# Graph attention, layer 1: the tile's sum enters each group's aggregation through an identity product, ScalarE copies it back, VectorE rescales, four message buffers

## What is computed

```python
h = (x @ W).reshape(n, NHEAD, OUT_FEATS)
h_l = (a_l * h).sum(-1)
h_r = (a_r * h).sum(-1)
e = h_l[row] + h_r[col]
e = jnp.where(e > 0, e, ALPHA * e)
m = jax.ops.segment_max(e, row, num_segments=n)
ex = jnp.exp(e - m[row])
denom = jax.ops.segment_sum(ex, row, num_segments=n)
att = ex / (denom[row] + 1e-16)
msg = att[:, :, None] * h[col]
out = jax.ops.segment_sum(msg, row, num_segments=n)
```

## Time and profile before

| | us |
|---|---|
| median of 3 runs | 2386.41 |
| lowest, highest | 2377.89, 2386.74 |
| span of the profiled execution | 2383.0 |

### The profile page before, as it was taken

How to read it: one execution, slowest core, us unless ns; L and a number is a source line. 1 busy time by engine, 2 the same in 40 slices (tenths; PEclk the granted TensorE clock), 3 DMA queues, 4 the chain that set the end, 5 groups by cost and what they waited for, 6 DMA issues and landing times.

```text
span 2383.0 us, 44547 instructions
## 1 busy us (share of the span) xinstructions
PE 1942.2 (82%) x9758; PEld 1420.1 (60%) x9759; DVE 1818.7 (76%) x4333; ACT 1484.5 (62%) x5321; POOL 1484.6 (62%) x1468
## 2 busy tenths in 40 slices
PE   0889999999928889888898899855778787878774
PEld 0457777777716777677777677632445454545442
DVE  7873333333348999999999999785889998999987
ACT  2236666666617777777778777446666666666660
POOL 3737777777777666666566656127666666666660
PEclk9999999999968999999999999987998989898997
DMA  8343333333329898888889885025434334343311
GB/s 238 127 179 131 131 131 129 131 131 130 123 92 328 291 298 292 300 295 297 297 287 304 302 292 174 4 60 133 106 105 106 105 105 107 99 112 100 108 37 54
DMA packets 162160, 403.34 MB, mean 169 GB/s; under 512 B 46887, under 2 KB 59099, under 8 KB 162108
## 3 DMA queue, kind: packets, MB, share of 16 engines
q0 software_dynamic: 79360, 276.09, 35.9%
q1 hardware_dynamic: 82748, 126.67, 16.8%
HBM read 343.89 MB, written 84.72 MB: 180 GB/s over the span
## 4 chain that ended last, share of the span: by engine, by line
PE 36%; DVE 25%; issue 15%; DMA 9%; POOL 7%; DVEq 3%; ACT 3%; ACTq 0%; SPq 0%; POOLq 0%
PE ps L1421 12%; DMA arena<-sorted_edges 6%; POOL sorted_edges L570 5%; PE ps L1454 4%; DVE gmx L1273 4%; PE ps L1457 4%; PE ps L1407 4%; PE ps L1469 3%; DVE arena L1305 2%; PE ps L1579 2%; DVE work L1268 2%; DVEq L334 2%; DVE arena L1102 2%; DVE sc L1116 2%; DMA arena<-node_row,idxC 2%
## 5 line engine op out<-in xcount | busy, mean ns | idle before, releaser
L639 POOL DMA_INDIRECT arena<-node_row,idxC x464 | 484.4, 1044 | 238.5 <-issue 132.6
L570 POOL DMA_INDIRECT sorted_edges<-work,idxA x416 | 417.3, 1003 | 146.7 <-issue 143.9
L1062 DVE TENSOR_TENSOR work<-ps,b_bc 128x512 f32<-128x512 f32 x208 | 143.9, 692 | 322.9 <-PE ps L1421 322.9
L1421 PE MATMUL ps<-w_sb,arena 128*128 128x256 f32 x1664 | 386.7, 385 | 0.0
L1579 PE MATMUL ps<-arena,hq 128*128 128x260 f32 x928 | 282.2, 432 | 86.5 <-DVE work L1268 81.1
L1421 PEld LDWEIGHTS ps<-w_sb,arena 128*128 128x128 f32 x1664 | 307.6, 190 | 72.0 <-issue 34.3
L594 POOL DMA_INDIRECT work<-node_kvx,idxB x232 | 244.5, 1054 | 156.6 <-DVE arena L1133 51.6
L594 POOL DMA_INDIRECT arena<-node_kvx,idxB x232 | 240.9, 1038 | 144.2 <-issue 53.4
L709 ACT ACTIVATE work<-work 128x256 f32<-128x256 f32 x416 | 188.7, 500 | 193.3 <-DVE work L1062 193.3
L1273 DVE TENSOR_REDUCE gmx<-ps 128x4 f32<-128x1024 f32 x232 | 283.1, 1220 | 31.5 <-PE ps L1554 31.5
L1454 PE MATMUL ps<-arena,work 128*128 128x256 f32 x928 | 255.6, 399 | 59.5 <-issue 40.6
(11 more groups left out here) (195 smaller groups left out, 3868.1 us busy)
## 6 DMA issues: line engine op xcount, KB each, us to landing
arena<-sorted_edges SPq DMA_DIRECT2D x232, 260.0 KB, 4.7
work<-sorted_rows SPq DMA_DIRECT2D x58, 256.0 KB, 3.5
arena<-in_edge_attr SPq DMA_DIRECT2D x25, 512.0 KB, 3.6
node_kvx<-arena SPq DMA_DIRECT2D x24, 384.0 KB, 2.3
arena<-node_row,idxC POOLq DMA_INDIRECT x464, 2.9
sorted_edges<-work,idxA POOLq DMA_INDIRECT x416, 2.4
sorted_edges<-arena SPq DMA_DIRECT2D x25, 260.0 KB
sorted_edges<-arena SPq DMA_DIRECT2D x1, 6240.0 KB
```

What stands on the lines that cost most here:

```text
L570: pool.indirect_dma_start(rec_dram[:, :], bass.IndirectOffsetOnAxis(ap=idxA[:, st.slot(8), c:c + 1], axis=0), recA[:, st.slot(8), c, :], N ...
L639: pool.indirect_dma_start(row1_g[:, st.slot(16), j, :], None, row1_dram[:, :], bass.IndirectOffsetOnAxis(ap=idxC[:, batch(st).slot(4), st. ...
L1421: ins = pe.matmul(ps[:, 5 + t, half * H:(half + 1) * H], hidT[:, r, m, half, t * P:(t + 1) * P], w2_sb[:, m, :], start=m == 0, stop=m == 1)
```

## The change

The tile's sum no longer meets the group's sum on VectorE. TensorE adds a third product to the group's aggregation, the identity times the tile's sum, in the same PSUM bank, so that the bank holds the new sum; ScalarE copies the bank to `acc1`. VectorE keeps only the rescaling, once in four groups. TensorE aggregates group s - 14 at step s, ScalarE copies group s - 15 at step s, and VectorE rescales for group s - 10. The message ring grows from two to four, with a semaphore of its own (`msg1_used`) that is set ahead of the identity product. TensorE and ScalarE now also read the tile numbers, twice in a turn each.

```diff
@@ scalar
                     act.copy(hrT[0:PARTS, pair(c).slot(2), :], trh).then_inc(s("hrT"), 1)
+                if st.u % 8 == 0:
+                    act_tiles[15] = tiles16(ACT_ENGINE, st.k, 15, st.u // 8)
+                d = st.back(15)
+                if d.real():
+                    act.wait_ge(s("agg1_ready"), d.n + 1)
+                    act.copy(acc1[:, bass.ds(act_tiles[15][st.u % 8], 1), :].rearrange("p a n -> p (a n)"),
+                             agg1[d.slot(2)]).then_inc(s("acc1_done"), 1)
...
-                        act.wait_ge(s("agg1_ready"), st.n - 15)
+                        act.wait_ge(s("msg1_used"), st.n - 15)
@@ vector
-                c = st.back(11)
-                if c.real():
-                    acc = tile(acc1, tiles[8][st.u % 8])
+                c = st.back(10)
+                if c.real() and c.u % BG == 0:
+                    acc, k = tile(acc1, tiles[10][st.u % 8]), batch(c)
+                    dve.wait_ge(s("mscale"), k.n + 1)
                     if not c.first(1):
                         dve.wait_ge(s("acc1_done"), c.n)
...
-                    dve.wait_ge(s("agg1_ready"), c.n + 1)
-                    dve.tensor_tensor(acc, acc, agg1[c.slot(2)], ALU.add).then_inc(
-                        s("acc1_done"), 1)
...
-                if st.u == 7:
-                    tiles[8] = tiles16(DVE, st.k, 11, 1)
+                if st.u % 8 == 0:
+                    tiles[10] = tiles16(DVE, st.k, 10, st.u // 8)
...
-                    if not m.first(2):
-                        dve.wait_ge(s("agg1_ready"), m.n - 1)
-                    dve.tensor_tensor(msg1[:, m.slot(2), :, :].rearrange("p c (h d) -> p c h d", d=HE),
+                    if not m.first(4):
+                        dve.wait_ge(s("msg1_used"), m.n - 3)
+                    dve.tensor_tensor(msg1[:, m.slot(4), :, :].rearrange("p c (h d) -> p c h d", d=HE),
@@ tensor
-                d = st.back(13)
+                if st.u % 8 == 0:
+                    pe_tiles[14] = tiles16(PE, st.k, 14, st.u // 8)
+                d = st.back(14)
                 if d.real():
...
                     for j in range(GJ):
-                        ins = pe.matmul(agg1[r], oneh1[:, r16, j, :], msg1[:, r, j, :],
-                                        start=j == 0, stop=j == GJ - 1)
-                    ins.then_inc(s("agg1_ready"), 1)
+                        ins = pe.matmul(agg1[r], oneh1[:, r16, j, :], msg1[:, r4, j, :],
+                                        start=j == 0, stop=False)
+                    ins.then_inc(s("msg1_used"), 1)
+                    if d.u % BG == 0:
+                        pe.wait_ge(s("acc1_scaled"), batch(d).n + 1)
+                    else:
+                        pe.wait_ge(s("acc1_done"), n)
+                    pe.matmul(agg1[r], ident[:, :],
+                              acc1[:, bass.ds(pe_tiles[14][st.u % 8], 1), :].rearrange("p a n -> p (a n)"),
+                              start=False, stop=True).then_inc(s("agg1_ready"), 1)
@@ gpsimd
-            pool.memset(hrT[:, :, :], 0.0).then_inc(s("acc1_zero"), 1)
             pool.wait_ge(s("acc0_done"), NG)
+            pool.memset(hrT[:, :, :], 0.0).then_inc(s("acc1_zero"), 1)
```

More of the change, by code:

```diff
@@ L256, in gnn_kernel @@
         row1_g = carve(16 * GJ * ROW1).rearrange("p (s c n) -> p s c n", s=16, c=GJ)
-        msg1 = carve(2 * GJ * NH1 * HE).rearrange("p (s c n) -> p s c n", s=2, c=GJ)
+        msg1 = carve(4 * GJ * NH1 * HE).rearrange("p (s c n) -> p s c n", s=4, c=GJ)
         hrT = carve(2 * 2 * GJ * P // 2).bitcast(BF16).rearrange("p (s n) -> p s n", s=2)
@@ L606, in _ @@
             pool.memset(gmx[:, :, :, 0:1], -BIG).then_inc(s("acc1_zero"), 1)
+            pool.wait_ge(s("acc0_done"), NG)
             pool.memset(hrT[:, :, :], 0.0).then_inc(s("acc1_zero"), 1)
-            pool.wait_ge(s("acc0_done"), NG)
             for r in range(4):
@@ L887, in layer1 @@
                     act.activation(mscale[:, r, :], mdiff[:, r, :], ACT.Exp).then_inc(s("mscale"), 1)
-            run(act, NG, 16, 9, layer1)
+            run(act, NG, 16, 15, layer1)
         @block.vector
@@ L1251, in layer1 @@
                 g, b = st.u % BG, batch(st)
-                if st.u == 0:
-                    tiles[8] = tiles16(DVE, st.k, 11, 0)
-                c = st.back(11)
-                if c.real():
-                    acc = tile(acc1, tiles[8][st.u % 8])
+                c = st.back(10)
+                if c.real() and c.u % BG == 0:
+                    acc, k = tile(acc1, tiles[10][st.u % 8]), batch(c)
+                    dve.wait_ge(s("mscale"), k.n + 1)
                     if not c.first(1):
                         dve.wait_ge(s("acc1_done"), c.n)
[L1259 to L1266, removed]
-                    dve.wait_ge(s("agg1_ready"), c.n + 1)
-                    dve.tensor_tensor(acc, acc, agg1[c.slot(2)], ALU.add).then_inc(
-                        s("acc1_done"), 1)
+                    dve.tensor_tensor(acc.rearrange("p (h d) -> p h d", d=HE),
+                                      acc.rearrange("p (h d) -> p h d", d=HE),
+                                      mscale[:, k.slot(2), :].unsqueeze(2).to_broadcast([P, NH1, HE]),
+                                      ALU.mult).then_inc(s("acc1_scaled"), 1)
                 if st.real():
@@ L1310, in layer1 @@
                     top(b, st)
-            run(dve, NG, 16, 11, layer1)
+            run(dve, NG, 16, 10, layer1)
             dve.wait_ge(s("acc1_done"), NG)
@@ L1569, in layer1 @@
                     ins.then_inc(s("hm_mm"), 1)
-                d = st.back(13)
+                if st.u % 8 == 0:
+                    pe_tiles[14] = tiles16(PE, st.k, 14, st.u // 8)
+                d = st.back(14)
                 if d.real():
-                    n, r, r16 = d.n, d.slot(2), d.slot(16)
+                    n, r, r16, r4 = d.n, d.slot(2), d.slot(16), d.slot(4)
                     pe.wait_ge(s("oneh1"), n + 1)
@@ L1578, in layer1 @@
                     for j in range(GJ):
-                        ins = pe.matmul(agg1[r], oneh1[:, r16, j, :], msg1[:, r, j, :],
-                                        start=j == 0, stop=j == GJ - 1)
-                    ins.then_inc(s("agg1_ready"), 1)
-            run(pe, NG, 16, 13, layer1)
+                        ins = pe.matmul(agg1[r], oneh1[:, r16, j, :], msg1[:, r4, j, :],
[8 more added lines that the diff above has]
+                              start=False, stop=True).then_inc(s("agg1_ready"), 1)
+            pe_tiles = {}
+            run(pe, NG, 16, 14, layer1)
 def run8(eng, total, body):
```

## The result

The changed kernel takes 2503.4 us (median of four runs, 2502.8 to 2509.5) against 2384.4 us before (four runs): the ratio is 1.0505, with a 95% interval of 1.0485 to 1.0525. It is 119 us slower; the prediction had 2513 us, 127 us slower.

A forecast was written before the change was run, and what follows sets the result against it. VectorE bounds the kernel before; afterwards a chain between ScalarE and TensorE does. Turns of 58.4 against 49.75 us, x 14.5, give 125 us, plus 2 for the drain: 127 us more, 2513 us, range 2400 to 2600.

The forecast's parts named there:

- if nothing else came late: VectorE's own work falls from 49.75 to some 42 us a turn; with no other delay the gain would be 109 us.
- The ring: TensorE's step s - 2, ScalarE's copy, one-hot and L853, TensorE's step s wait in turn: two passages, 12.40 us a batch.
- first passage: Into step 4k: identity product's end, ScalarE's copy, one-hot, mask, L853, then TensorE's step to its product's end: 7.47 us.
- second passage: Into step 4k + 2, the same way without the mask: 2.09 on ScalarE, 0.16, 2.68 on TensorE, 4.93 us.
- table reads, a turn: Tile-number reads, twice a turn: 1.9 us each on TensorE, nothing more on ScalarE, 3.8 us a turn.
- clock, a turn: TensorE idles 2.4 us a batch and its clock then halves: 1.2 us lost a batch, 4.8 a turn.
- a turn: 16 groups, four batches: 53.6 us with table reads and loop, 58.4 with the clock loss, against 49.75 before.
- the turn's head: The loop's own time in each turn of 16 groups: 0.2 us.
- The rescaling: VectorE stands ahead of L1262 for ScalarE's copy, 2 to 3 us a batch, which it has to spare: covered.
- (a): Ring holds but TensorE's clock stays up or its loss is covered: turn 53.6 us, +58 us, 2444 us; chance 0.28.
- (b): ScalarE's queue is less late, next busiest engine sets the pace: turn 46.2 us, -51 us, 2335 us; chance 0.12.
- Buys nothing then: The message ring of four brings no gain after the change, since the wait isn't at VectorE.

The follow-up runs named there:

- the fastest kernel: ScalarE's copy and VectorE's rescaling each one step later, against the changed kernel: 2354.4 us, ratio 0.9871 to the kernel before.

## Why the prediction was right

**The bound before.** VectorE set the pace: shortening its addition alone gave 35 us. But something else was nearer behind it than the 109 us of "if nothing else came late" would need.

**The ring.** This is the cause. The order of instructions in ScalarE's queue (49 us for moving the copy behind the one-hot), the work in that queue (71 us against 8 for the same instruction after and before) and the lag of the copy (73 us) all move the time, and none of the three changes TensorE's amount of work. The terms, at full clock, in us:

| term | predicted | measured |
|---|---|---|
| product's end to L853's end, first passage | 4.42 | 4.44 |
| ScalarE to TensorE | 0.16 | 0.05 |
| TensorE's step 4k | 2.89 | 2.97 |
| first passage | 7.47 | 7.46 |
| second passage | 4.93 | 4.85 |
| a batch | 12.40 | 12.31 |
| table reads, a turn | 3.8 | 2.7 |
| clock, a turn | 4.8 | 4.5 |
| a turn | 58.4 | 58.11 |

The measured turn is the distance from the L1536 at 2069.77 to the one 16 groups earlier:

```profile
2011.66 0.59 PE L1536 MATMUL ps<-ident_b,arena 128*12 128x128 bf16 x4 [2.79 <-ACT arena L853]
...
2027.12 0.39 PE L1536 MATMUL ps<-ident_b,arena 128*12 128x128 bf16 x4 [2.31 <-ACT arena L853]
...
2041.10 0.38 PE L1536 MATMUL ps<-ident_b,arena 128*12 128x128 bf16 x4 [2.38 <-ACT arena L853]
```

Its four batches take 15.46, 13.98, 15.87 and 12.80 us. It is a typical one: ten turns from the L1536 at 1750.29 us to the one at 2331.23 take 58.09 us each. The last batch has full clock and no read: 12.31, and 0.48 for the turn's head, by which the hole at 2069.77 is longer (2.79 against 2.31); I had 0.2 for that head. (58.11 - 49.75) x 14.5 = 121 us, against 119 measured.

The clock and read terms in the table come from experiments that take each away alone, and so they don't add up: 49.2 + 0.5 + 2.7 + 4.5 = 56.9 leaves 1.2 us a turn. Taken one after the other they come closer. At full clock a turn should be 49.2 + 0.5 + 2.8 for the reads = 52.5, and with the hole filled it is 53.06; from there to 58.09 the clock takes 5.0. (The 4.5 is less, as it spreads the gain over the first turn too, whose holes were not filled.) About 0.5 us a turn stays without a name.

That the turn came out within 0.3 us is partly luck. The reads were 1.0 too high and the head 0.3 too low; within the first passage the time from product to copy was 0.14 and not 0.04, and the time from ScalarE to TensorE 0.05 and not 0.16. The order of the instructions, both passages and the size of the clock's loss were not luck.

**The clock.** Taking 15 of 19 holes as marked was close: of the 47 holes of 2.1 to 2.8 us ahead of L1536 between 1766 and 2431 in the changed kernel, 38 had the clock at 0.5 within two us of them. The 9 others all stand ahead of the fourth batch of a turn. The granted clock was to be "at or below 0.90", and is 0.85.

**The rescaling.** I had called it covered, with VectorE at rest 2 to 3 us a batch, which is what the trace shows (73.9 us in 32 waits, 2.3 each). That holds for the changed kernel, and the 4 us of the later rescaling agree with it. What I had not said is that it is a ring just behind the first: with only the copy later the kernel still stays above the kernel before.

**The rivals.** (a), the clock without effect, falls, as filling the hole gave 65 us; as a price for the ring alone its 2444 us was good. (b), the pace of the next busiest engine, is what is approached once both rings are loose: 2354 us, where I had 2335. The rule of the Trainium skill, "Perfetto Trace Analysis", section "Identifying the Most-Contended Engine", to optimize the engine with the highest occupancy first, picks the right engine here: 35 us by the short addition. It says nothing of the order in which the relief is queued, and that decided the sign. The Trainium skill, "Perfetto Trace Analysis", section "Optimization Strategy", says of consistent bubbles, the same gap repeating on the engine that should be saturated, that they can mean too little SBUF or PSUM for the next tile. TensorE's hole of 2.3 to 2.8 us in every batch repeats like that. Here the later copy and rescaling removed it with the same buffers (149 us).

**What was not tried.** The hole ends with L853, the copy out of PSUM bank 0, and TensorE's even step waits for it because the transposed logits have only this bank. A second bank for them would let TensorE run on past that wait, and might have opened the ring without any later lag. It would have to be found first: of the other seven, 1 to 4 hold the spreading, 5 and 7 are `agg1`, and 6 holds the small products. No run tests it.

**The message ring.** "Buys nothing then" is not tested for the changed kernel, but as a rule it was too broad: with two buffers the fastest kernel loses 112 us.

## What to carry to other kernels

When a step moves from a busy engine to one with time to spare, look at what stands behind it in the new queue and who waits for that: 35% idle time didn't help, because behind the copy's wait 4.4 us of ScalarE's queue stood between two steps of TensorE. Write out each chain that runs through two engines' programs back to its start, price it from start to start, and compare it with the busiest engine's turn. If it is longer, change the lags before the work, and loosen all chains of about the same length together: here a step each on two of them turned 5% slower into 1.3% faster, and either one alone stayed slower than the kernel before.

## What I had not expected of the hardware

Work without a result made the program faster: eight products of 512 bf16 columns in a hole of 2.3 us kept TensorE at 2.4 GHz (granted clock 0.99 against 0.85) and gave 65 us. The two table reads on TensorE cost 2.7 us a turn together with their fellows on ScalarE, while TensorE's idle time ahead of the next instruction showed 1.0; with a read the aggregation started 3.08 us after the step at half clock as at full clock. ScalarE's result reached TensorE in 0.05 us (L853's end at 2056.92, L1536 at 2056.97), and TensorE's product reached ScalarE's copy 0.14 us after its modelled end.
